# Pyramid-pooled attention on one core: the last two batches' order, and a tile's four projections in one run

## The reference

```python
qk = relu(bn(conv1x1(x, qk_w)))          # 512 -> 256 channels, x is 8 x 512 x 64 x 64
val = relu(bn(conv1x1(x, v_w)))          # 512 -> 512 channels
key, value = psp(qk), psp(val)           # max over grids of 1, 3, 6 and 8 squared cells: 110
scores = softmax(query @ key * 256 ** -0.5)        # query is qk, one row for each pixel
y = conv1x1(scores @ value, out_w)
return x + bn(y)
```

## Time and profile before

| | us |
|---|---|
| Runs (3): median, lowest to highest | 1422.11, 1422.07 to 1423.21 |
| The profiled execution | 1424.07 |
| its span, first to last record | 1422.4 |
| PE busy | 1386.1 (97%) |
| DVE busy | 847.2 (60%) |
| POOL busy | 498.1 (35%) |
| ACT busy | 485.1 (34%) |
| DMA queue q1, share of 16 engines | 42.4% |

### The profile page before, as it was taken

One profiled execution on the slowest core, in us unless ns is written; L12 is line 12 of the kernel. 1 busy time (PEld: TensorE's weight loads), 2 busy tenths in 40 slices (PEclk: granted clock), 3 DMA queues, 4 the chain that ended last, 5 costly groups with the idle time before them and its releaser, 6 DMA issues.

```text
span 1422.4 us, 15781 instructions
## 1 busy us (share of the span) xinstructions
PE 1386.1 (97%) x6029; PEld 1132.4 (80%) x6029; DVE 847.2 (60%) x1767; ACT 485.1 (34%) x681; POOL 498.1 (35%) x219
## 2 busy tenths in 40 slices
PE   7999999999999999999999999999999997999997
PEld 5888888888888888888888888888888885777875
DVE  6434655557645666557655666546665557676567
ACT  4112333332333323333323323423323424663430
POOL 2233323423423423323333323333333334664520
PEclk9999999999999999999999999999999998999998
DMA  5113234434434425434434434435435335786426
GB/s 193 60 59 99 80 109 158 171 125 148 155 132 158 172 99 174 149 136 159 139 133 173 154 132 159 140 130 175 153 114 177 138 133 189 248 288 221 145 89 237
DMA packets 107165, 213.38 MB, mean 150 GB/s; under 512 B 3370, under 2 KB 3410, under 8 KB 107090
## 3 DMA queue, kind: packets, MB, share of 16 engines
q1 hardware_dynamic: 106514, 211.32, 42.4%
q10 hardware_dynamic: 576, 1.05, 0.2%
HBM read 145.25 MB, written 67.11 MB: 149 GB/s over the span
## 4 chain that ended last, share of the span: by engine, by line
PE 90%; DVE 5%; POOL 3%; ACT 1%; issue 1%; DMA 0%; SPq 0%; ACTq 0%; DVEq 0%
PE conv_ps L349 23%; PE conv_ps L347 23%; PE conv_ps L348 23%; PE out_ps L389 3%; PE out_ps L388 3%; PE out_ps L390 3%; POOL xl L297 2%; PE score_ps L362 2%; PE score_ps L363 2%; PE score_ps L364 2%; POOL q_l L303 1%; PE sum_ps L375 1%; PE sum_ps L374 1%; DVE q L766 1%; ACT xh L503 1%
## 5 line engine op out<-in xcount | busy, mean ns | idle before, releaser
L347 PE MATMUL conv_ps<-xh,wh 128*128 128x512 f32 x1536 | 602.7, 392 | 0.0
L349 PE MATMUL conv_ps<-xl,wh 128*128 128x512 f32 x1536 | 602.0, 392 | 0.0
L348 PE MATMUL conv_ps<-xh,wl 128*128 128x512 f32 x1536 | 599.2, 390 | 0.0
L672 DVE TENSOR_REDUCE row_max<-conv_ps 128x64 f32<-128x512 f32 (+2 forms) x576 | 283.9, 530 | 418.0 <-ACT q L524 228.2
L297 POOL TENSOR_TENSOR xl<-xa,xh 128x1024 fp32r<-128x1024 f32 x142 | 342.0, 2413 | 446.5 <-ACT xh L503 446.5
L349 PEld LDWEIGHTS conv_ps<-xl,wh 128*128 128x128 f32 x1536 | 289.1, 188 | 64.0
L348 PEld LDWEIGHTS conv_ps<-xh,wl 128*128 128x128 f32 x1536 | 289.4, 188 | 63.1
L347 PEld LDWEIGHTS conv_ps<-xh,wh 128*128 128x128 f32 x1536 | 289.2, 188 | 61.4
L303 POOL TENSOR_TENSOR q_l<-q,q_h 128x1024 fp32r<-128x1024 f32 x64 | 154.9, 2420 | 423.4 <-ACT q_h L530 423.4
L524 ACT ACTIVATE q<-conv_ps,shift 128x512 f32<-128x512 f32 x128 | 88.2, 689 | 289.5 <-PE conv_ps L349 289.5
L535 ACT ACTIVATE score_ps<-score_ps 128x512 f32<-128x512 f32 x56 | 32.6, 582 | 438.9 <-PE score_ps L364 438.9
(11 more groups left out here) (165 smaller groups left out, 951.3 us busy)
## 6 DMA issues: line engine op xcount, KB each, us to landing
xa<-x SPq DMA_DIRECT2D x73, 1024.0 KB, 7.4
xo<-x SPq DMA_DIRECT2D x58, 1024.0 KB, 5.2
out<-xo SPq DMA_DIRECT2D x58, 1024.0 KB, 4.2
q<-x SPq DMA_DIRECT2D x4, 1024.0 KB, 5.4
out<-q SPq DMA_DIRECT2D x4, 1024.0 KB, 4.8
q<-v_w ACTq DMA_DIRECT2D x4, 256.0 KB, 4.5
xa<-x SPq DMA_DIRECT2D x2, 512.0 KB, 5.9
q<-out_w SPq DMA_DIRECT2D x1, 1024.0 KB, 7.5
```

The source lines that it names most:

```text
L347: nc.tensor.matmul(bank(s, c)[:, :], wh[:, k, cols], hi, start=(k == 0), stop=False)
L348: nc.tensor.matmul(bank(s, c)[:, :], wl[:, k, cols], hi, start=False, stop=False)
L349: last = nc.tensor.matmul(bank(s, c)[:, :], wh[:, k, cols], lo, start=False, stop=(k == KC - 1))
L672: last = nc.vector.tensor_reduce(row_max[:, c, n, :], src[:, r0_ * W:r1_ * W].rearrange("p (r w) -> p w r", w=W), AX.X, ALU.max)
```

## The change

**Ordinary steps (s < 56).** On PE the four projections stand in one run behind `conv(s, 2)`, then the scores, and in a step that begins a batch the projections of the values; then `conv(s, 3)`, `conv(s, 4)`, `conv(s, 5)`. Before, two projections stood behind `conv(s, 2)`, the scores behind `conv(s, 3)`, the other two projections (and those of the values) behind `conv(s, 4)`. On DVE all four `add_out` stand between `pool_rows(s, 1)` and `pool_rows(s, 2)`.

**Steps 56 to 63.** In step 56 PE has `conv(56, 4)`, `conv(56, 5)`, two projections and `conv(57, 4)` ahead of the scores. From step 57 on, `split_q_hi` (ACT) and `split_q_lo` (POOL) of the next tile stand ahead of the splits of x.

**Steps 64 to 71 and the end.** In step 64 the scores move behind `conv(64, 2)`. In step 71 `sums(62)` and `scores(63)` leave the step: the scores go between the projections of the values, `sums(62)` ahead of the row of projections, `sums(63)` behind those of tile 58. Of each tile from 56 to 62, output group 1 is copied out of PSUM by ACT (`copy_out`) and added by POOL (`add_copy`) in place of DVE's `add_out`.

```diff
@@ gpsimd
             for s in range(X):
+                if LAST < s < S:
+                    split_q_lo(s - (NT - 1))
                 if s + 1 < X:
                     split_lo(s + 1, 0)
                     split_lo(s + 1, 1)
-                if NT - 1 <= s < X - 1:
+                if NT - 1 <= s < X - 1 and not LAST < s < S:
                     split_q_lo(s - (NT - 1))
+            for a in range(LAST, S - 1):
+                add_copy(a)
@@ tensor, s < LAST
                 conv(s, 1)
                 conv(s, 2)
                 if ap >= 0:
-                    project(ap, 0)
-                    project(ap, 1)
-                conv(s, 3)
+                    for m in range(OC):
+                        project(ap, m)
                 if ac >= 0:
                     scores(ac)
+                    if ac % NT == 0:
+                        for m in range(VC):
+                            project_values(ac // NT, m)
+                conv(s, 3)
                 conv(s, 4)
-                if ap >= 0:
-                    project(ap, 2)
-                    project(ap, 3)
-                if ac >= 0 and ac % NT == 0:
-                    for m in range(VC):
-                        project_values(ac // NT, m)
                 conv(s, 5)
@@ tensor, s == LAST
                     conv(s, 4)
+                    conv(s, 5)
+                    project(ap, 0)
+                    project(ap, 1)
+                    conv(s + 1, 4)
+                    scores(ac)
+                    for m in range(VC):
+                        project_values(ac // NT, m)
+                    project(ap, 2)
+                    project(ap, 3)
+                    continue
@@ tensor, the end
             for m in range(VC - 1):
                 project_values(B - 1, m)
-            sums(S - 1)
+
+            scores(S - 1)
             project_values(B - 1, VC - 1)
+            sums(S - 2)
             for a in range(LAST, S):
                 for m in range(OC):
                     project(a, m)
+                if a == LAST + 2:
+                    sums(S - 1)
@@ scalar, the end
+            exps(S - 1)
+            guess(S - 2)
+            copy_out(LAST)
+            split_p_hi(S - 2)
+            copy_out(LAST + 1)
+            copy_out(LAST + 2)
+            guess(S - 1)
@@ vector, s < LAST
                 pool_rows(s, 1)
+                if ap >= 0:
+                    for m in range(OC):
+                        add_out(ap, m)
                 pool_rows(s, 2)
-                if ap >= 0:
-                    add_out(ap, 0)
-                    add_out(ap, 1)
-                pool_rows(s, 3)
...
                 if ac >= 0:
                     split_e_lo(ac)
-                pool_rows(s, 4)
-                if ap >= 0:
-                    add_out(ap, 2)
-                    add_out(ap, 3)
                 if last_of_batch:
                     make_values(ac // NT)
+                pool_rows(s, 3)
+                pool_rows(s, 4)
                 pool_rows(s, 5)
```

More of the change, by code:

```diff
@@ L213, in residual, with copied, copy_of, added @@
             return [xo[:, 0, :, :], xo[:, 1, :, :], q2[0], q2[1], q2[2], xa[:, 0, :, :], q2[3], xa[:, 1, :, :]][a - LAST]
+        COPIED = 1
+        def copied(a, m):
+            return LAST <= a < S - 1 and m == COPIED
+        def copy_of(a):
+            if a % 2:
+                return row_max[:, :, :, :].rearrange("p c n w -> p (c n w)")[:, 0:TN]
+            return cells[:, :, :].rearrange("p c n -> p (c n)")[:, 0:TN]
+        def added(a, m):
+            n = OC * a + m + 1
+            if a >= LAST:
+                n -= min(a, S - 1) - LAST + (1 if a < S - 1 and m >= COPIED else 0)
+            return n
         @block.sync
@@ L458, in _ @@
                 project(ap, 1)
-                if s == LAST:
-                    for m in range(VC):
-                        project_values(ac // NT, m)
-                    project(ap, 2)
-                    project(ap, 3)
             for s in range(S, X):
                 ap, ac = s - NT - 1, s - NT
-                sums(ap)
+                if s < X - 1:
+                    sums(ap)
                 if s == S:
@@ L830, in _ @@
                 normalise(ap)
-                if s == LAST + 1:
-                    values_lo(ap // NT)
                 if s == LAST:
@@ L840, in _ @@
                     split_e_lo(ac)
-                else:
-                    split_e_lo(ac)
-                    if s > LAST + 1:
-                        add_out(ap - 1, 2)
-                    split_p_lo(ap)
-                    if s > LAST + 1:
-                        add_out(ap - 1, 3)
+                    pool_rows(s, 5)
+                    add_out(ap, 0)
+                    add_out(ap, 1)
+                    make_values(ac // NT)
+                    pool_cells(s, VC, CC)
+                    pool_rows(s + 1, 4)
+                    add_out(ap, 2)
+                    add_out(ap, 3)
+                    continue
+                if s == LAST + 1:
+                    values_lo(ap // NT)
+                split_e_lo(ac)
+                if s > LAST + 1:
+                    add_out(ap - 1, 2)
+                split_p_lo(ap)
+                if s > LAST + 1:
+                    add_out(ap - 1, 3)
                     pool_cells(s - 1, VC, CC)
@@ L889, in _, with add_outs @@
             last_values_lo(3)
-            for m in range(OC):
-                add_out(LAST, m)
+            def add_outs(a):
+                for m in range(OC):
+                    if not copied(a, m):
+                        add_out(a, m)
+            add_outs(LAST)
+            split_e_lo(S - 1)
+            refine(S - 2)
+            add_outs(LAST + 1)
+            normalise(S - 2)
+            add_outs(LAST + 2)
+            split_p_lo(S - 2)
+            add_outs(LAST + 3)
             refine(S - 1)
             normalise(S - 1)
-            for m in range(OC):
-                add_out(LAST + 1, m)
+            add_outs(LAST + 4)
             split_p_lo(S - 1)
-            for a in range(LAST + 2, S):
-                for m in range(OC):
-                    add_out(a, m)
+            for a in range(LAST + 5, S):
+                add_outs(a)
 def kernel(x, L0_conv_qk_w, L0_conv_qk_gamma, L0_conv_qk_beta, L0_conv_qk_mean, L0_conv_qk_var,
```

82 lines of the change are left out of this document (57 added, 25 removed).

## The result

| | before | after |
|---|---|---|
| Median of the runs, us | 1422.64 (4 runs, 1422.07 to 1423.21) | 1465.28 (4 runs, 1461.42 to 1465.78) |
| The profiled execution, and its span | 1424.07, 1422.4 | 1465.09, 1463.3 |

The ratio of the times is 1.0294, with an interval of 1.0275 to 1.0312: the change makes the kernel slower by 2.9%. The sign was forecast; the size was not. The forecast was 1454 with a range up to 1463.

The account below looks back on a forecast made before the run. PE was taken as the bound, busy for 97% of the span. +16.8 + 22.8 + 10 + 2.2 (step 8) - 4.7 - 15 = +32.1 us on the median 1422.11 gave 1454 us, range 1440 to 1463.

Parts of the forecast that it names:

- The sign: Whole kernel: the change makes it slower, chance 0.90, against 0.03 for the same and 0.07 for faster.
- (a): Middle steps: no stall, the additions come in time, giving 1404.6 us, faster; chance 0.07.
- (b): Middle steps: only the short stalls come, the long ones are hidden, giving 1421.4 us, no change; chance 0.03.
- (c): Middle steps: the stalls come without the fall of the clock, giving 1444 us; chance 0.12.
- the ordinary steps' wait: 42 ordinary steps: project(a, 2) waits 0.40 us for add_out(a, 0), 16.8 us more (14 to 21).
- the saved runs: Steps 9 to 55: two fewer runs of attention matmuls save 0.10 us a step, 4.7 us off.
- the start-up: Ahead of step 8: no term in the sum, forecast difference 0.
- the last batches' gain: Step 56 to the end: shorter waits and a quicker end gain 15 us (bounds 9 and 19).
- the batch steps' clock: Steps 16, 24, 32, 40, 48: clock falls behind each long wait, 2.0 us each, 10 us (bounds 0 and 13).
- Batch steps, +1.6: Steps 16, 24, 32, 40, 48: project(a, 2) loses 4.55 us waiting for DVE, 22.8 us, with 10 us of clock on top.
- From span to median: Whole kernel: the median before lies 1.96 us below the profiled execution, so the forecast time is 1422.11 + 32.1.
- (d): Steps from 58: residuals land later than the additions want them, 1 us in each of six steps, 1460 us; chance 0.08.

Follow-up runs that it names:

- Batch steps old: The changed kernel with the order of before on PE and DVE in steps 0 to 7 and the batch-beginning steps: 1425.75 us, ratio 1.0020.
- filler: The changed kernel with 18 more matmuls on PE ahead of project(a, 2) in each batch step, filling the wait: 1452.93 us.
- scores between: The changed kernel with the scores (and the values' projections) between projections 0, 1 and 2, 3, still in one run: 1420.36 us, ratio 0.9989.
- end only: The changed kernel's steps 56 to 71 and end, with the kernel before's order in steps 0 to 55: 1408.10 us, ratio 0.9896.
- exponentials first: The best kernel with POOL's split_q_lo(49) put off until the values in step 56, and ACT's exps(48) ahead of store_q(57, 0): 1402.79 us, ratio 0.9863.
- values first: The changed kernel with POOL's second split of x in batch steps 16 to 48 put off until DVE made the values' halves: 1449.34 us.
- best kernel: The changed kernel with old order in steps 0 to 7 and batch steps, ordinary steps' scores between projections, and project(56, m)'s bank wait mended: 1404.91 us.

## Why the prediction was right or wrong

**The sign and the mechanism were right.** That PE would wait for the banks' additions, about 45 times shortly and five times for 4.4 us, that the clock would fall five times in the middle, and that DVE's 54-element addition in step 56 would take over 2 us: all of it is in the trace. POOL and DVE in step 56 of the kernel after (before, the addition took 0.22 us):

```profile
1235.84 2.47 POOL L333 TENSOR_TENSOR q_l<-q,q_h 128x1024 fp32r<-128x1024 f32 x1
```

```profile
1236.05 2.33 DVE L785 TENSOR_TENSOR cells<-rows 128x54 f32<-128x54 f32 x1
```

Rivals (a), (b) and (c) are gone by the trace of the kernel after: 49 waits, 4.66 us in a batch step, a granted clock of 0.50 behind it. Batch steps old, filler and scores between then price the short waits (0.38 us net), the clock (2.49) and the bank's distance.

**The size was not, and the time came out above the range.** On the spans the sum was +32.1 us and the difference +41.0, 8.9 more. The steps that failed are terms of the sum. The largest miss is the ordinary steps' wait less the saved runs, put at 16.8 - 4.2 = 12.6 us and measured at 15.8; the start-up stood at nothing without a reason and took 2.1; the last batches' gain was put at 15 and is 13.0; the batch steps' clock at 10 and took 11.3. One by one, the first four with what they add to the 8.9:

- *Ordinary steps, +3.2.* The step failed twice in the same direction. The wait was worked out at 0.42 and taken as 0.40, by rows of another wait; it is 0.34 + 0.10 = 0.44 to 0.45 (start to start 1.71, which was exact, and 0.33 to the second matmul, where 0.31 was read). Two runs fewer were taken as 0.10 and save 0.07. The price of a run was worked out as a remainder over four runs, 0.21 / 4; two fewer gave back a third of the remainder, not half. Net +0.377 a step (x 42 = 15.8) for +0.30. The bounds (0.34 to 0.50) held it.
- *Batch steps, +1.6.* Together they took 33.9 us more than before for 32.3. Typical are 4.47 us of standing for 4.45, and 2.49 us of clock for 2.0, 11.3 for 10 in all five. I counted 12 matmuls at +0.20 from the row of before and then took 2.0 without a row for the discount; the uncut 2.4 was right in four of five steps (the first lost 1.5).
- *Start-up, +2.1, missed.* The prediction says nothing on step 0. The change moves `pool_rows(s, 3)` to behind the later work of DVE's step, in step 0 too, where that work is the scaling of the output weights, for whose halves PE waits. That is a part of the diff that was not costed.
- *The last batches, +2.0.* The term was 15 us, and the run end only gained just that in its trace. The kernel after gained 13.0: the clock fell in step 56 (7 matmuls) and once at the end (5), and in end only at neither place. That end only has just 15 is in part luck: it gains 10.9 us in steps 56 to 63, where 12.0 were forecast, and 4.0 behind them, where 3.0 were. `project(56, 2)` and `project(56, 3)` wait for one addition too many, 1.7 us that I had missed, and in the kernel after DVE waited 1.0 us for DMA. So other steps gained more than I gave them; one of these is a stretch of 7 matmuls at half clock at 1391 us of the trace before, which is gone with the new end and which I had not counted.
- *From span to median, +2.* The forecast went from the profiled execution of before (1424.07) to its median by taking off 1.96. The profiled execution of after stands at its own median (1465.09 to 1465.28). Step 8 begins at 147.9 to 149.2 us in eight traces with the same order in step 0, so start-ups alone differ by over 1 us, and one profile's distance from its median is no property of the kernel. The range should have had this at its upper end: the time lies 2.3 us above it, and this or the missed start-up makes up nearly all of that.

**On the clock the forecast was surer than its rows.** It rested on one fall behind a wait of 7.4 us and one wait of 2.5 us without a fall. For the 4.7 us here that was enough. As a sign that 2.5 us are safe it was not: the counts at the end of this text have falls behind waits of 2.3 to 2.7 us from start to start, where this one is 2.9.

**Rival (d), DMA, came in small.** It was put at 1 us in each of six steps; it was 1.0 us once, at the end of step 63. In the other traces with the new end DVE's waits for the residual sum to between 0 (filler, exponentials first) and 3.2 us (values first). The kernel after, SP's queue, then DVE:

```profile
1301.19 0.37 SPq L245 DMA_DIRECT2D xo<-x  x1
...
1312.16 0.37 SPq L245 DMA_DIRECT2D xo<-x  x1
```

```profile
1317.51 1.29 DVE L842 TENSOR_TENSOR xo<-out_ps,xo 128x512 f32<-128x512 f32 x2 [0.95 <-DMA xo<-x]
```

Steps 58 to 63 now take 10.07 us on PE, but the residual's loads are issued every 10.7 to 11.0 us (four intervals, 1268.73 to 1312.16), since each waits until the store of two tiles earlier has landed. A step moves three transfers of 1024 KB; that in 10.9 us is 289 GB/s, and the stretch 1260 to 1310 shows 282 at a DMA share of 0.83. So the loads fall behind by 0.8 us a step, and the slack lasts until step 63. The wait there differs from kernel to kernel (`project(54, 2)` starts 0.66 us behind the matmul ahead of it in the filler's trace, 2.5 to 2.6 in three others). No run here slows or speeds the transfers, so that they set this pace is read from the rows and not tested.

## What to carry to other kernels

Before matmuls are brought together, count what stood between the two uses of each bank. Two interruptions fewer were worth 0.07 us a step here, and the bank's round trip (matmul, addition, next matmul: 1.71 us) costs whatever of it is no longer covered; other work of PE put between the uses keeps the saving and loses the wait. Look at the steps in which the releasing engine has something long ahead of the release, since there the same reordering cost some eighteen times as much (6.96 us for 0.38, both net), and at the first step, where it moves setup work too.

When an operation is postponed, follow who overwrites what it reads: putting off POOL's split made ACT wait to overwrite its input, which gave back all of the 2.1 us; moving one line on ACT kept them. And when an operation on POOL holds up one on DVE, look at the whole row behind it: put off past one, it held up another.

## What the runs showed of the hardware that was not expected

**Only behind the longest waits did the clock fall every time.** Counted over the traces of all kernels here by the time from one matmul's start to the next, behind step 8: of 20 waits of 4.6 to 4.8 us and two of 7.8, all 22 were followed by a stretch at the lower level; of ten waits of 3.0 us in step 56, seven; of the five of 2.6 us in the run values first, three; of 12 waits of 2.3 us in the last projections, five; of six others between 2.3 and 2.9 us, one; and one of 3.7 us was not (two of 2.4 us, with a further wait close behind, are not counted). The same kernel's place can go either way, so a forecast with such a wait needs both values. Behind such a wait 5 to 12 matmuls take 0.427 instead of 0.227 us, a loss of 1.0 to 2.4 us.

**The fall can come after PE has started again.** The first matmuls of the best kernel's scores in step 56, on PE:

```profile
1182.53 0.50 PE L402 MATMUL score_ps<-q_h,key_h 128*128 128x512 f32 x1 [2.64 <-DVE key_l L816]
...
1183.33 0.40 PE L402 MATMUL score_ps<-q_h,key_h 128*128 128x512 f32 x1
1183.57 0.54 PE L403 MATMUL score_ps<-q_h,key_l 128*128 128x512 f32 x1
1183.91 0.63 PE L404 MATMUL score_ps<-q_l,key_h 128*128 128x512 f32 x1
```

PE stood for 2.64 us, took up work at 0.23 us a matmul, and went to 0.43 about 1.1 us later. Whoever looks at the wait's own stretch alone does not see this fall; it stands in the stretch behind.
